# First batch of an attention and ternary feed-forward kernel: a new order for VectorE's and GpSimd's side work

## The reference

```
xn = layernorm(x)                                   # x: 8 batches of 512 x 256
q, k, v = mlp_q(xn), mlp_k(xn), mlp_v(xn)           # gelu(xn @ W1 + b1) @ W2 + b2, all 256 wide
s = layernorm((tril(q @ k.T / scale)) @ v) * ln_w + ln_b
quantize(W) = clip(round(W / (mean(|W|) + 1e-5)), -1, 1)
h = relu(xn @ quantize(W1).T + b1)                  # 1024 wide
g = silu(h @ quantize(W2).T + b2)
out = x + s * g
```

## Time and profile before

| | us |
|---|---|
| median of 3 runs | 307.65 |
| lowest, highest | 307.64, 307.9 |
| the profiled execution, its own time | 307.09 |
| span of the profiled execution, first to last instruction | 305.4 |
| TensorE busy in it | 299.8 (98%) |
| TensorE's share of the chain that ended last | 89% |
| VectorE busy | 247.6 (81%) |
| ScalarE busy | 222.4 (73%) |
| GpSimd busy | 133.7 (44%) |
| mean granted TensorE clock, share of full | 0.999 |

### The profile page before, as it was taken

The page is one execution under the profiler, slowest core; times in us unless marked ns, Lnnn a source line. Parts: engine busy times, 40 slices in busy tenths (PEclk is TensorE's granted clock), DMA queues, the critical chain, the costliest instruction groups (busy, mean ns, idle before and its releaser), DMA issues.

```text
span 305.4 us, 5730 instructions
## 1 busy us (share of the span) xinstructions
PE 299.8 (98%) x1856; PEld 268.7 (88%) x1856; DVE 247.6 (81%) x546; ACT 222.4 (73%) x429; POOL 133.7 (44%) x105
## 2 busy tenths in 40 slices
PE   8999999999999999999999999999999999999995
PEld 7878899889988899888997889888998889988895
DVE  4989798967999589976999669995799858696686
ACT  3696948966786857949489576877679494895862
POOL 3945835167060942429151580609515291404200
PEclk9999999999999999999999999999999999999999
DMA  7970044510007000240004200070001500020001
GB/s 235 375 217 2 1 140 137 166 43 2 1 2 206 0 0 0 58 149 0 0 0 143 64 0 0 1 206 1 0 0 32 174 0 0 0 71 2 0 2 69
DMA packets 15228, 19.06 MB, mean 62 GB/s; under 512 B 1776, under 2 KB 12528, under 8 KB 15216
## 3 DMA queue, kind: packets, MB, share of 16 engines
q1 hardware_dynamic: 14656, 18.51, 19.2%
q10 hardware_dynamic: 560, 0.40, 0.4%
HBM read 14.69 MB, written 4.22 MB: 62 GB/s over the span
## 4 chain that ended last, share of the span: by engine, by line
PE 89%; DVE 4%; DMA 3%; SPq 2%; ACT 1%; issue 0%; POOL 0%; DVEq 0%
PE bank L860 87%; DMA x_all<-in_w1t 3%; DVE g L666 1%; SPq L201 1%; DVE gw L780 1%; DVE gw L658 1%; DVE x_all L660 0%; PE bank L974 0%; DVE gw L809 0%; PE bank L975 0%; DVE w1q L611 0%; ACT r_lo L408 0%; PE bank L972 0%; SPq L212 0%; PE bank L844 0%
## 5 line engine op out<-in xcount | busy, mean ns | idle before, releaser
L756 DVE TENSOR_TENSOR r_lo<-bank,r_hi 128x512 fp32r<-128x512 f32 x64 | 44.0, 691 | 34.8 <-ACT bank L471 34.6
L470 ACT ACTIVATE r_hi<-bank,col 128x512 fp32r<-128x512 f32 x64 | 47.0, 734 | 24.6 <-PE bank L860 24.6
L471 ACT ACTIVATE bank<-bank,col 128x512 f32<-128x512 f32 x64 | 45.4, 710 | 0.0
L367 POOL TENSOR_TENSOR o_rstd<-o_var,neg_half 128x2 f32<-128x2 f32 x16 | 11.2, 699 | 76.2 <-ACT o_var L504 76.2
L322 POOL TENSOR_TENSOR y<-y,xn 128x512 f32<-128x512 f32 x12 | 19.7, 1643 | 56.4 <-DMA y<-in_x_t 56.4
L860 PE MATMUL bank<-xT_lo,w1q 128*128 128x512 f32 x128 | 39.5, 390 | 0.0
L860 PE MATMUL bank<-xT_hi,w1q 128*128 128x512 f32 x128 | 39.5, 390 | 0.0
L449 ACT ACTIVATE g<-bank,col 128x512 fp32r<-128x512 f32 x48 | 34.3, 714 | 1.0 <-PE bank L860 0.9
L860 PE MATMUL bank<-w2q,r_lo 128*128 128x256 f32 x256 | 34.6, 278 | 0.0
L860 PE MATMUL bank<-w2q,r_hi 128*128 128x256 f32 x256 | 34.3, 276 | 0.0
L450 ACT ACTIVATE bank<-bank,col 128x512 f32<-128x512 f32 x48 | 33.1, 689 | 0.0
(11 more groups left out here) (150 smaller groups left out, 686.5 us busy)
## 6 DMA issues: line engine op xcount, KB each, us to landing
out<-x_all SPq DMA_DIRECT2D x15, 256.0 KB, 3.1
x_all<-in_x SPq DMA_DIRECT2D x7, 512.0 KB, 3.5
xn<-x_norm_rows SPq DMA_DIRECT2D x6, 512.0 KB, 4.2
y<-in_x_t SPq DMA_DIRECT2D x6, 512.0 KB, 4.8
x_all<-in_w1t SPq DMA_DIRECT2D x2, 512.0 KB, 7.8
x_all<-in_w2t SPq DMA_DIRECT2D x1, 1024.0 KB, 10.4
row<-in_rows SPq DMA_DIRECT2D x1, 512.0 KB, 4.7
x_all<-in_x SPq DMA_DIRECT2D x1, 256.0 KB, 3.2
```

The lines of the kernel that those rows point to most:

```text
L367: nc.gpsimd.tensor_tensor(o_rstd[:, half], o_var[:, half], neg_half[:, half], ALU.pow).then_inc(o_rstd_made, 1)
L470: nc.scalar.activation(r["hi"][:, f], pre[:], ACT.Relu, bias=b1)
L471: nc.scalar.activation(pre[:], pre[:], ACT.Relu, bias=b1).then_inc(f1_whole, 1)
L756: nc.vector.tensor_tensor(r["lo"][:, f], bank[(AT_F1 + f) % BANKS][:], r["hi"][:, f].bitcast(FP32), ALU.subtract).then_inc(r_split, 1)
```

## The change

On VectorE, `quantise1(0)` moves from behind g_lo(1) to behind g_lo(5), directly ahead of `quantise1(1)`; `thresholds(0)` moves to behind g_lo(3), and `thresholds(1)` moves ahead, from behind v's additions to behind `quantise1(1)`. On GpSimd, the parts of e and the bias row go ahead of `xn1_tile`, behind a new wait for all six g_lo (`g_split` 6), and `quantise_rest` waits for W2's flags (`flags_made` 3) instead of VectorE's whole part of W2 (`w2_quantized` 1). No instruction that computes is added or removed.

```diff
             def batch(i, first=False, second_last=False, last=False):
                 if first:
+                    pool.wait_ge(g_split, 6)
+                    pool.wait_ge(e_made, 1)
+                    nc.gpsimd.tensor_copy(e["hi"][:], e32[:]).then_inc(e_hi_made, 1)
+                    pool.wait_ge(e_hi_made, 1)
+                    nc.gpsimd.tensor_tensor(e["lo"][:], e32[:], e["hi"][:].bitcast(FP32),
+                                            ALU.subtract).then_inc(e_split, 1)
+                    pool.wait_ge(v_shift_made, CK + 1)
+                    nc.gpsimd.tensor_scalar(row[:, ROW_B2V], row[:, ROW_B2V], v_shift[:, CK:CK + 1], None,
+                                            ALU.add).then_inc(v_centred, 1)
                     pool.wait_ge(x_rstd_made, 1)
                     pool.wait_ge(xT_summed, 2 * CK)
                     pool.wait_ge(w1_quantized, 1)
                     xn1_tile(0)
                     xn1_tile(1)
-                    pool.wait_ge(v_shift_made, CK + 1)
-                    nc.gpsimd.tensor_scalar(row[:, ROW_B2V], row[:, ROW_B2V], v_shift[:, CK:CK + 1], None,
-                                            ALU.add).then_inc(v_centred, 1)
-                    pool.wait_ge(e_made, 1)
-                    nc.gpsimd.tensor_copy(e["hi"][:], e32[:]).then_inc(e_hi_made, 1)
-                    pool.wait_ge(e_hi_made, 1)
-                    nc.gpsimd.tensor_tensor(e["lo"][:], e32[:], e["hi"][:].bitcast(FP32),
-                                            ALU.subtract).then_inc(e_split, 1)
-                    pool.wait_ge(w2_quantized, 1)
+                    pool.wait_ge(flags_made, 3)
                     quantise_rest()
...
+                g_lo(2)
+                g_lo(3)
                 if first:
                     thresholds(0)
+                g_lo(4)
+                g_lo(5)
+                if first:
                     dve.wait_ge(thr_made, 2)
                     quantise1(0)
-                g_lo(2)
-                g_lo(3)
-                g_lo(4)
-                g_lo(5)
-                if first:
                     dve.wait_ge(w1_quantized, 1)
                     quantise1(1)
+                    thresholds(1)
                     dve.wait_ge(w1_quantized, 2)
...
                 if first:
-                    thresholds(1)
                     dve.wait_ge(e_split, 1)
                     quantise2()
```

More of the change, by code:

```diff
@@ L695, in batch @@
                     finish(i - 1, 2, 2, 2)
+                g_lo(2)
+                g_lo(3)
                 if first:
                     thresholds(0)
-                    dve.wait_ge(thr_made, 2)
-                    quantise1(0)
-                g_lo(2)
-                g_lo(3)
                 g_lo(4)
@@ L704, in batch @@
                 if first:
+                    dve.wait_ge(thr_made, 2)
+                    quantise1(0)
                     dve.wait_ge(w1_quantized, 1)
                     quantise1(1)
+                    thresholds(1)
                     dve.wait_ge(w1_quantized, 2)
```

## The result

The changed kernel takes 310.58 us (median of 4 runs, 310.34 to 310.79) where the kernel before takes 307.70 in the same runs: ratio 1.0088, 95% interval 1.0070 to 1.0106. Its profiled execution took 310.49 us with a span of 308.7. The change costs about 2.9 us; 310.3 was predicted.

What follows compares the result with a forecast made beforehand. TensorE, busy for 98% of the span, was taken as the bound. Delays from GpSimd and VectorE excluding each other on SBUF put its third sum 2.62 us late: 307.65 + 2.62 = 310.3 us, range 306.8 to 310.9.

Steps and rivals of the forecast that it cites:

- v's wait: TensorE's wait ahead of v's first product in the first batch: its lost 0.80 us would all be gained.
- The parts of e beside W1: GpSimd's e_hi and e_lo would delay VectorE's quantising of W1 by 0.30 and 1.0 us.
- with no collision: If GpSimd and VectorE didn't hold each other off, VectorE would reach quantise2's end at about 31.5 us.
- B: Rival, 0.20: v_lo doesn't get between L764's halves; only W2's rest is late, 308.7 us, or 307.7 without e's collision.
- C: Rival, 0.22: L312 runs beside L611, e's parts fit in, and the 0.80 us gain stays: 306.85 us.
- L312 behind L611: GpSimd's first step on W2's rest is kept out by VectorE until 32.29 us; the earlier release buys only 0.13.
- W2's rest: GpSimd's share of quantising W2 is whole at 38.71 us, so TensorE's ffn_out starts 1.01 us later than before.
- L764: VectorE's pair is held off by L316, then cut in two by v_lo; its second half begins 3.33 us later.
- The scores' low parts: They come late behind L764; the third delays TensorE's third sum to 46.85 us, 2.62 us later than before.
- v_lo's hold: v's low part on GpSimd runs from 38.86 to 41.26 us and holds VectorE off until 41.13.
- Behind this all shifts as one: After the third sum, all later work moves with TensorE, so the 2.62 us is carried to the end.
- D: Rival, 0.10: GpSimd starts L312 ahead of L611, or TensorE's new gaps cost more: 308.5 to 311 us.

Runs made afterwards that it cites:

- e7: e8 with GpSimd's xn1_tile(1) and a wait for w2_quantized put between L312 and the rest of W2's work; 0.9980 of the kernel before.
- e9: e7 run once more, unchanged, on another chip; 0.9986 of the kernel before.
- e4: The changed kernel with W2's rest on GpSimd waiting for w2_quantized again instead of the flags; 1.0089 of the kernel before.
- e5: The changed kernel with v's low part on GpSimd also waiting for both halves of L764; 1.0054 of the kernel before.
- e10: The changed kernel run again, on the same chip as e9; 1.0098 of the kernel before.
- e6: e3 without the wait for W2's flags, so W2's rest on GpSimd waits only for the thresholds; 1.0056 of the kernel before.
- e3: The changed kernel with GpSimd's parts of e put back behind xn1_tile and the bias row; 1.0059 of the kernel before.
- e8: e6 with v's low part on GpSimd also waiting for both halves of L764; 1.0003 of the kernel before.

## Why the prediction was right

- **v's wait.** 0.80 us, g_lo(5) ready with 0.57 to spare: right. It was ready at 22.18 for a product at 22.74, and e7 and e9 keep 0.77 and 0.72 of it.
- **The parts of e beside W1.** +0.30 and +1.0 were taken, 0.23 and 0.92 measured (L612 1.51 for 1.28, L610 1.67 for 0.75). quantise2 was to end at 32.42 and ended at 32.54, in an execution that ran 0.25 late from its start (20.02 for 19.77). One sum beside this was wrong: quantise2's end "with no collision" isn't 31.5 but, by the prediction's own terms, 32.42 less 1.30, 31.1; e7, with holds of 0.2 and 0.1 left, reached 31.32. The forecast doesn't use it. Rivals B (without e's collision) and C do: by 31.1 B's 307.7 would have been some 0.3 less, and C's time the same.
- **L312 behind L611.** About 3.6 us long was expected, 3.58 measured; the gain of the early wait was put at 0.13 us and is 0.22 by e4's rows. The 0.13 left out the 0.10 that GpSimd needs from W2's semaphore to L312 and that the prediction itself read; its time for W2 had it in.
- **W2's rest.** +1.01 us at `ffn_out`; 39.06 - 37.75 less the 0.25 is +1.06.
- **L764.** 3.33 us late was expected. The pair is 3.25 longer than naturally, of which e5 gives 2.09 to v_lo and leaves 1.16 to L316; the expected shares were 2.27 and 1.33. As it also started 0.35 early after the 0.25 are taken off, its end is 2.9 late.
- **The scores' low parts.** As forecast, TensorE waits for the first three, and the third decides: the third sum starts at 46.68, just behind its low part. Counted from start to start, the first, second and third sum come 0.30, 0.60 and 0.24 later than they followed before. Less the 0.25, the third is 2.20 late where 2.62 was reckoned; at the end of the measure it is +2.39 and +2.27 in two executions. The terms that were too large are L764's place and v_lo's hold.
- **The end.** "Behind this all shifts as one" was wrong by some tenths. The median moved by 2.88 us (in e10 by 3.25), the profiled span by 3.3. What lies between 2.39 and 3.3 is 0.25 from the late start and about 0.66 from batches 2 and 5, where TensorE steps more slowly (last section). Nothing that the change does was found behind the 0.5 to 1.0 us by which the medians moved more than the first batch, and the executions they come from have no trace. So the mechanism was right and its sum 0.2 to 0.4 too large; that the median came within 0.3 us of the forecast is in part luck.
- **The rivals.** B (v_lo doesn't cut in) is what e5 makes by adding a wait: +1.37. C had its argument in L338, which let L611 pass after 0.09 us; that argument is right for one side only. e6 and e7 show that a GpSimd tensor_scalar holds VectorE off just at its beginning, 0.63 us of 2.25 for 768 columns, but is itself held off for as long as VectorE works. D didn't occur: L612 was first, by 0.06 us.

The Trainium skill's rule in Advanced Engine Details and Errata, VectorE Performance Modes, that two-port VectorE instructions and GpSimd's block each other, is borne out by e3, e5 and e6 as far as the blocking goes: without the meeting L609 fell from 1.67 to 0.93 us and the pair of L764 from 3.98 to 1.89, or from 2.79 to 0.72 (e8). No run shows which of VectorE's instructions use two ports.

## What to carry to other kernels

Work that is moved to an idle engine isn't moved to idle ports: where GpSimd and VectorE both work on SBUF, look up in the trace what each instruction will lie beside, and put GpSimd's tensor_tensors beside VectorE work that reads PSUM. A busy time that has grown with nothing changed in the instruction was, in each case here, a wait that the waits view doesn't name. And a side task that only just missed a collision before (here L316 ended 0.17 us ahead of L764) has to be counted among the costs of being late.

## What the runs showed of the hardware

**A hold differs by form.** GpSimd's tensor_tensor of 512 columns held VectorE for 1.13 us of 1.30, that of 1024 for about 2.1 of 2.44 (e5), a tensor_scalar of 768 columns for 0.63 of 2.25 (e6) and not at all once it had run for 0.74 us (e7: started 28.12, VectorE's at 28.86 took its natural 0.88). The other way round no such difference was seen: GpSimd's tensor_scalar L312 waited 1.36 us beside L612 and its tensor_tensor e_lo 0.85 us, both until about 0.13 us before the printed end of VectorE's instruction.

**TensorE's pace.** In the changed kernel's profile the groups of eight 128x256 products follow each other every 0.91 us in batch 1 and every 0.94 us in batch 2 (start, busy time):

```profile
78.06 1.07 PE L861 MATMUL bank<-w2q,r_hi 128*128 128x256 f32 x8
78.97 1.07 PE L861 MATMUL bank<-w2q,r_lo 128*128 128x256 f32 x8
...
113.97 1.11 PE L861 MATMUL bank<-w2q,r_hi 128*128 128x256 f32 x8
114.92 1.11 PE L861 MATMUL bank<-w2q,r_lo 128*128 128x256 f32 x8
```

The granted clock is 1.00 in both stretches. It makes such a batch some 0.2 to 0.4 us longer: from one batch's score tail to the next it was 35.91 us without it and 36.15 with it, in the changed kernel's batch 5 36.22. e9 had it in most of its batches, and for that its profile has a span of 306.3 although its first batch gained as much as e7's. What decides it wasn't tried and stays open. It may be a part of the scatter between executions that made the intervals wide; they have no trace that could show it.

**A start that differs.** TensorE begins with 34 products of ones, 128x128 each, in front of the first batch. They take 5.51 us in the profile of before, 6.42 in that of the changed kernel and 6.93 in e10's, where z's first product starts at 19.77, 20.02 and 20.53. They follow each other every 0.21 us at first and every 0.11 later, and the step comes after 14, 23 and 28 of them. Nothing that the change moves has run by then, so this is scatter of the start and no part of what the change costs.
